# Second layer's transposes, derivative, keys, queries and values as one block with split products, and one preparation of expert weights less

## The reference, cut to what matters

```
exp_out = einsum('blef,edf->bled', gelu(einsum('bld,efd->blef', x, w1) + b1), w2) + b2   # first layer
...
lap_x = yp_x[:, :, :-2] - 2.0 * y + yp_x[:, :, 2:]      # second difference along the features
lap_y = yp_y[:, :-2, :] - 2.0 * y + yp_y[:, 2:, :]      # second difference along the tokens
du_dt = zX * lap_x + zY * lap_y + zR * y * (1.0 - y)
q, k, v = du_dt @ Wq.T, du_dt @ Wk.T, du_dt @ Wv.T      # then 4 heads, each with two softmaxes
...
```

## Time and profile before

| what | us |
|---|---|
| three runs | 1522.03, 1523.15, 1525.40 (median 1523.15) |
| the profiled execution, its own time | 1524.83 |
| its span (first to last instruction) | 1523.0 |
| busy: PE, DVE, ACT, POOL | 1372.9, 943.2, 722.7, 497.7 |
| last job's last VectorE instruction ends | 978.9 |
| last preparation on GpSimd ends | 983.6 |
| transposes of the second layer begin | 985.4 |
| `laplace_phase` begins | 991.8 |
| attention begins | 1053.8 |

### The profile page before, as it was taken

How to read it: one execution, slowest core, us unless ns; L and a number is a source line. 1 busy time by engine, 2 the same in 40 slices (tenths; PEclk the granted TensorE clock), 3 DMA queues, 4 the chain that set the end, 5 groups by cost and what they waited for, 6 DMA issues and landing times. The chain is left out here.

```text
span 1523.0 us, 24894 instructions
## 1 busy us (share of the span) xinstructions
PE 1372.9 (90%) x8678; PEld 1139.8 (75%) x8679; DVE 943.2 (62%) x1708; ACT 722.7 (47%) x1473; POOL 497.7 (33%) x478
## 2 busy tenths in 40 slices
PE   8866799978998789999999999888899899867998
PEld 3345356667895479999999999736688688647997
DVE  4955879965566854454343343395777777464776
ACT  3423877635122246555445556312555456333543
POOL 0331089830000234274062040442211210043885
PEclk9976989989998969999999999999999999988999
DMA  6000000010000014021011000050000000533550
GB/s 235 1 1 0 14 1 1 1 56 1 1 1 0 1 60 162 0 99 67 0 50 60 0 0 0 0 166 1 1 1 1 1 1 1 194 120 115 193 198 20
DMA packets 23244, 69.50 MB, mean 46 GB/s; under 512 B 4419, under 2 KB 8915, under 8 KB 18242
## 3 DMA queue, kind: packets, MB, share of 16 engines
q1 hardware_dynamic: 20866, 62.51, 11.8%
q0 software_dynamic: 2304, 6.03, 1.1%
HBM read 54.62 MB, written 14.19 MB: 45 GB/s over the span
## 5 line engine op out<-in xcount | busy, mean ns | idle before, releaser
L1702 DVE TENSOR_TENSOR ehidl<-hT,ehidh 128x512 fp32r<-128x512 f32 x148 | 140.4, 960 | 136.5 <-ACT ehidh L1685 135.9
L1679 ACT ACTIVATE hT<-ps,eb 128x256 f32<-128x256 f32 x296 | 124.4, 472 | 165.8 <-PE ps L1521 165.8
L2010 ACT ACTIVATE pr<-ps,nmax 128x256 f32<-128x256 f32 (+7 forms) x128 | 94.1, 739 | 103.4 <-DVE nmax L2040 103.3
L1521 PE MATMUL ps<-kh,qz 128*128 128x512 f32 (+3 forms) x384 | 125.3, 380 | 3.3 <-ACT pr L2010 1.9
L1709 DVE SCALAR_TENSOR_TENSOR X<-ps,wE,X 128x256 f32 x74 | 35.8, 484 | 108.3 <-PE ps L1521 98.7
L1685 ACT CAST ehidh<-hT 128x512 fp32r<-128x512 f32 x148 | 91.9, 621 | 4.7
L2040 DVE TENSOR_REDUCE nmax<-ps 128x1 f32<-128x256 f32 (+7 forms) x128 | 91.0, 748 | 1.2 <-PE ps L1950 0.6
L1603 POOL TENSOR_TENSOR eb<-eb1s,consts 128x8 f32<-128x8 f32 x8 | 2.1, 260 | 273.6 <-PE ps L1521 267.3
L1521 PEld LDWEIGHTS ps<-kh,qz 128*128 128x128 f32 x384 | 76.2, 199 | 13.3 <-ACT pr L2010 4.7
L1521 PE MATMUL ps<-ew_1h,ehidh 128*128 128x256 f32 x304 | 85.5, 281 | 0.5 <-POOL ew_1l L1623 0.5
L1521 PE MATMUL ps<-hTh,ew_1h 128*128 x304 | 85.4, 281 | 0.1
(11 more groups left out here) (524 smaller groups left out, 4303.1 us busy)
## 6 DMA issues: line engine op xcount, KB each, us to landing
ew1s<-in_ew_dram SPq DMA_DIRECT2D x9, 1024.0 KB, 4.7
ew2s<-in_ew_dram SPq DMA_DIRECT2D x9, 1024.0 KB, 6.8
fw1s<-in_fw_dram SPq DMA_DIRECT2D x8, 1024.0 KB, 7.6
fw2s<-in_fw_dram SPq DMA_DIRECT2D x8, 1024.0 KB, 9.4
slot_rows<-fill SPq DMA_DIRECT2D x1, 5140.0 KB, 20.1
xr<-slot_rows SPq DMA_DIRECT2D x8, 514.0 KB, 4.1
xT<-in_xT_dram SPq DMA_DIRECT2D x4, 512.0 KB, 7.6
X<-in_x_dram SPq DMA_DIRECT2D x1, 2048.0 KB, 18.2
```

The lines of the kernel that those rows point to most:

```text
L1521: last = nc.tensor.matmul(out, lhs[a], rhs[b], start=(start and n == 0), stop=(stop and n == 2), **kw)
L1679: nc.scalar.activation(hid[:, f, :], ps[:, f // 2, (f % 2) * JOB:(f % 2 + 1) * JOB], ACT.Gelu, bias=b1[q][:, f:f + 1]).then_inc(k.e_act, 1)
L1702: nc.vector.tensor_tensor(lo[:, f, :], hid[:, f, :], hi[:, f, :], ALU.subtract).then_inc(k.e_lo, 1)
L2010: nc.scalar.activation(pr[:, n % 3, u, 0:wide], half(n, u, wide), ACT.Exp, bias=nmax[:, n % 2, u:u + 1], accum_out=sums[:, u, n:n + 1]).th ...
```

## The change: what it does, and the diff

1. **Mixture.** GpSimd and SP handle expert 1 ahead of the loop, and the loop runs over max(pairs − 1, 1) further pairs, 2p+2 and 2p+3. With four pairs, GpSimd makes 7 preparations in place of 8 and SP one load less of each weight.
2. **One block.** The call of `transpose_phase` goes; `laplace_phase` does the transposes itself, window by window, and ScalarE alone copies them out (`stream`).
3. **Split products.** The stream, du, wk, wq and wv are each cut into high and low parts, and TensorE works with fp32r passes: four per second difference (2 halves × high and low; the constant matrix has one part), six per group of keys or queries (2 × `product3`) and twelve half-wide ones per group of values. The parts of the stream and of du share the buffers qh and ql, which the queries' parts later take.
4. **Who does what.** ScalarE makes all high parts and the growth factor (`growth`, z0·y + z1), and copies out the values, two tiles at once. VectorE makes low parts, the product with y, the neighbour sums (now straight from hT, `neighbours`) and the rest of du. GpSimd makes the weights' low parts first, clears a third of `qz` and the filler, waits for the last low part of du, clears the rest and places the queries.
5. **Order.** On PE, ACT and DVE the order is written out call by call; windows overlap.

```
-            return (p * 2 + 1, 1, p + 1) if q == 0 else (p * 2 + 2, 0, p + 2)
+            return p * 2 + (q + 2), q, p + 2
+        def later_pairs(eng, name):
+            rest = eng.alloc_register(f"{name}_later_pairs")
+            eng.reg_alu(rest, entry(eng, "pairs", 0, E0 // 2), -1, ALU.add)
+            eng.reg_alu(rest, rest, 1, ALU.max)
+            return eng.snap(rest, min_val=1, max_val=E0 // 2 - 1)
...
-            with pool.Fori(0, pairs) as p:
+            split(1, 1, 1)
+            with pool.Fori(0, rest) as p:
                 for q in range(2):
                     split(*following(p, q))
...
+            def second_difference(w, f):
+                pe.wait_ge(k.l_lap, 1)
+                pe.wait_ge(k.l_yl, EB * (w + 1))
+                for j in range(EB):
+                    for n in range(2):
+                        last = nc.tensor.matmul(ps[:, bank(w, f), :], lap[:, j * E + f * P:j * E + (f + 1) * P],
+                                                parts[n][:, j, window(w)], start=(j == 0 and n == 0),
+                                                stop=(j == EB - 1 and n == 1))
+            def keys(w, f):
+                pe.wait_ge(k.l_wl, SPLIT.index(KEY) + 1)
+                pe.wait_ge(k.l_dl, EB * (w + 1))
+                weighted(w, f, wk, k.l_km)
...
+            def high_weight(n):
+                act.wait_ge(k.s_wC, 16 * 4)
+                nc.scalar.copy(PARTS[n][0][:, :, :], WHOLE[n][:, :, :]).then_inc(k.l_wh, 1)
+            high_weight(0)
+            stream(0, 0)
+            high(0, 0)
+            stream(0, 1)
+            growth(0)
...
+            low_weight(0)
+            low_weight(2)
+            low_weight(1)
+            clear(0)
             nc.gpsimd.memset(k.fill[:, 0:ROWF - 1], 0.0).then_inc(k.z_fill, 1)
             nc.gpsimd.memset(k.fill[:, ID].bitcast(I32), OUTSIDE).then_inc(k.z_fill, 1)
+            pool.wait_ge(k.l_dl, EB * NW)
+            for q in range(1, QZ):
+                clear(q)
             pool.wait_ge(k.z_fill, 2)
-            pool.wait_ge(k.l_zero, 1)
+            pool.wait_ge(k.l_zero, 2 * QZ)
             pool.wait_ge(k.l_ql, EB)
             for i in range(QZ):
                 place_queries(nc, k, i)
...
+            def neighbours(w):
+                def add(at, of, n):
+                    o = du[:, :, first + at:first + at + n]
+                    then(nc.vector.scalar_tensor_tensor(o, k.hT[:, :, first + of:first + of + n], k.row("zy", b), o,
+                                                        ALU.mult, ALU.add))
...
-                transpose_phase(nc, k, k.X, k.hT, None, None, {"mm": k.t_5})
                 laplace_phase(nc, k)
```

More of the change, by code:

```diff
@@ L1762, in _ @@
[L1762 to L1782, removed]
-                last.then_inc(k.l_vm, 1)
+            def turn(w, f):
+                for j in range(4):
+                    last = nc.tensor.transpose(ps[:, bank(w, f), j * P:(j + 1) * P],
+                                               k.X[:, 4 * w + j, f * P:(f + 1) * P], k.const("ident"))
+                last.then_inc(k.t_5, 1)
@@ new lines, in weighted @@
+            def weighted(w, f, weight, done):
+                for j in range(EB):
+                    last = product3(nc, ps[:, bank(w, f), :], [x[:, j, f * P:(f + 1) * P] for x in weight],
+                                    [x[:, j, window(w)] for x in parts], j == 0, j == EB - 1)
+                last.then_inc(done, 1)
+            def keys(w, f):
+                pe.wait_ge(k.l_wl, SPLIT.index(KEY) + 1)
+                pe.wait_ge(k.l_dl, EB * (w + 1))
+                weighted(w, f, wk, k.l_km)
@@ new lines, in _ @@
+            second_difference(2, 1)
+            keys(1, 0)
+            keys(1, 1)
+            queries(0, 1)
+            second_difference(3, 0)
+            second_difference(3, 1)
+            values(1, 0)
+            keys(2, 0)
+            keys(2, 1)
+            queries(1, 0)
+            values(1, 1)
+            values(2, 0)
+            queries(1, 1)
+            keys(3, 0)
+            keys(3, 1)
+            queries(2, 0)
+            values(2, 1)
+            values(3, 0)
+            queries(2, 1)
@@ L1785, in _ @@
+            values(3, 1)
+            queries(3, 0)
+            queries(3, 1)
         @block.scalar
         def _(act):
[L1787 to L1802, removed]
+            def stream(w, f):
+                act.wait_ge(k.t_5, EB * w + f + 1)
+                nc.scalar.copy(k.hT[:, f, window(w)], ps[:, bank(w, f), :]).then_inc(k.l_ya, 1)
+            def high(w, f):
+                act.wait_ge(k.l_ya, EB * w + f + 1)
+                nc.scalar.copy(k.qh[:, f, window(w)], k.hT[:, f, window(w)]).then_inc(k.l_yh, 1)
@@ new lines, in _ @@
+            coefficients()
+            low(0, 0)
+            growth(0)
+            low(0, 1)
+            neighbours(0)
+            differences(0, 0)
+            differences(0, 1)
+            low(1, 0)
+            growth(1)
+            low(1, 1)
+            low_derivative(0, 0)
+            low_derivative(0, 1)
+            neighbours(1)
+            low_keys(0, 0)
+            differences(1, 0)
+            low(2, 0)
+            low_keys(0, 1)
+            low(2, 1)
+            growth(2)
```

272 lines of the change are left out of this document (203 added, 69 removed).

## The result

The changed kernel takes **1515.56 us** (median of five runs, 1513.12 to 1517.56) against 1523.15 (median of five as well): a ratio of 0.9951, with a 95% interval of 0.9939 to 0.9963, so 7.6 us less (5.6 to 9.3). Forecast were 1513.6 and a range of 1508.0 to 1519.5.

The account below looks back on a forecast made before the run. TensorE's list was taken to bound most of the program, with POOL alone holding the seam. 4.7 us at the seam plus 4.8 in the stretch (68.1 to 63.3) gave 9.5 off 1523.15: 1513.6 us, range 1508.0 to 1519.5.

Parts of the forecast that it names:

- Part 1: Seam behind the mixture: without POOL's unused last preparation, VectorE is last out, 4.7 us earlier; the following 1.8 us stay.
- Leg A: Block's start: ScalarE's first cast waits for four weight loads, so VectorE's first low part starts at 7.6 us.
- R3: Rival, walk too careful: loads land 1 us sooner, VectorE's waits vanish, block ends at 58.6, time 1508.9 us; chance 0.11.
- Leg B: VectorE's list up to window 2's derivative low parts: 27.8 us of work plus 3.7 of waits, ending at 39.1.
- The 1.1 for growth: VectorE's wait of 1.1 us behind ScalarE's growth step, which stands ahead of the next high part.
- the 1.6 at window 1's low part: VectorE's wait of 1.6 us for a high part made after growth and a weight cast, and against POOL's weight parts.
- a full lock: POOL's three weight low parts hold VectorE for their whole length, 3.7 us in place of 1.6; end at 65.4.
- Leg C: TensorE's last 15 groups, from keys(2, 0) on: 20.7 us plus 0.7 of waits, 21.4, ending at 60.7.
- R4: Rival, slower: TensorE stays at 1.2 GHz through its last 15 groups, 41.4 us for 20.7, result 1534; chance 0.04.
- Leg D: Block's end: POOL's placing of queries, 10.5 us from 52.7, ends last at 63.3, 0.5 us behind the rest.
- R2: Rival: the new lists mesh worse than the walk; the stretch takes 67.9 us, time 1518.2; chance 0.14.

Follow-up runs that it names:

- the block alone: The changed kernel with the mixture's old loops, so the preparation that no job reads is back: 1520.71 us, ratio 0.9971 to the kernel before.
- the second execution: The changed kernel unaltered, timed and profiled once more: 1516.99 us, ratio 0.9948 to the kernel before.
- the later cast: The changed kernel with ScalarE's cast of wk moved behind the copies of windows 0 and 1: 1513.34 us, ratio 0.9927 to the kernel before.
- The earlier placing: The changed kernel with ScalarE's high part of window 0's second half of queries moved ahead of the last two keys: 1515.01 us in one run.
- the last kernel: The changed kernel with wk's cast later, the queries step earlier, and 18 and 50 unused transposes in TensorE's pauses: 1510.17 us, ratio 0.9902 to the kernel before.

## Why the prediction held, step by step

**Part 1, the seam: 4.7 us.** Right to a tenth, and by its reason: the 1.8 us behind the last engine stayed, behind VectorE in each of the eleven profiled executions without the last preparation (1.76 to 1.77) and behind POOL in the block alone (1.79).

**Leg A: VectorE's first low part at 7.6.** It came at 6.5. The 4.4 us for the last load were carried over from the earlier trace rows; measured were 3.4 and, in the second execution, 4.2. This term was mis-sized by 1.0 us in one execution and 0.2 in the other. With 3.4 one half of R3 came true: ScalarE began 4.7 us behind the first transpose, before the 5 us that stood as R3's sign. The other half, that the waits vanish, did not. That the loads stand on the path is shown by the later cast (A from 6.5 to 1.9). Window 0's second difference began 10.4 and 11.2 us behind the first transpose, for 11 to 12.

**Leg B: 27.8 of work and 3.7 of waits.** VectorE's window has 28.3 of work in 31.1 us; 31.5 were forecast. The 1.1 for growth came out at 1.10. Of the 1.6 at window 1's low part only contention came true, 0.41 of lengthening: its high part was ready, and VectorE didn't wait for it. The 0.38 of idle time just ahead belong to the step on PSUM at 992.83, which waited for TensorE's second difference, whose passes stood 0.43 apart:

```profile
992.16 0.63 PE L1775 MATMUL ps<-ql,lapr 128*128 128x512 f32 x1
```
```profile
992.83 0.75 DVE L2015 SCALAR_TENSOR_TENSOR att<-ps,rows,att 128x512 f32<-128x512 f32 x1 [0.38 <-PE ps L1775]
```

**Contention.** VectorE's steps with two SBUF inputs were held (1.10 for 0.69; 4.75 for 2.86 with the cast later), its step on PSUM was not (0.75 at 991.70, under POOL's weight part), and the placing took 10.5 us, six sets of 1.70 or 1.71. That is the pattern of the Trainium skill (SBUF — State Buffer, "Who interferes with whom"), and this case's traces agree with it. The page excepts steps with one SBUF input in a 2-port mode, which the prediction left out when it told the rule, and the kernel before has steps with one SBUF input that were held:

```profile
991.83 3.59 DVE L1853 TENSOR_SCALAR zc<-rows 128x2 f32<-128x2 f32 x1 [0.31 <-PEq L434]
...
995.65 3.88 DVE L1831 TENSOR_SCALAR att<-hT,zc 128x512 f32<-128x512 f32 x1
...
1001.75 3.90 DVE L1831 TENSOR_SCALAR att<-hT,zc 128x512 f32<-128x512 f32 x1
...
1007.88 0.54 DVE L1831 TENSOR_SCALAR att<-hT,zc 128x512 f32<-128x512 f32 x1
```
```profile
995.65 3.59 POOL L1809 TENSOR_TENSOR nb<-hT 128x2044 f32<-128x2044 f32 x1
```

The 512-wide step takes 0.54 alone, and the one of two columns 0.17 in the changed kernel. The third was held by the clearing of `qz`, which only writes (999.66 to 1004.87). So some 10 of the 16.0 us in which the earlier trace rows show VectorE busy were holding, and "nearly full" was a misreading. The change takes this away: `growth` moves that step to ScalarE, and the neighbour sums and most of the clearing leave that stretch. A smaller edit, the kernel before with this step on ScalarE alone, was not run. An estimate from rows: at most the 2.3 us of TensorE's pause at 1005.8 (it waits there for du of window 0) and half of the 3.7 us at half clock, so some 4 us, near to the 4.4 that the new block gains in its second profile. Whether the new block was needed for its gain is therefore open.

The 3.7 us that the prediction allowed for by a full lock fell to 0.4. Of the three weight parts one met hardly any such step, one was held itself (2.18), and only the last held a low part; with GpSimd given the neighbour sums, the steps held, the waits for it and half clock made the block 4 to 6 us longer.

**Leg C: 21.4 us without half clock.** It took 21.5 (1016.59 to 1038.05), and 21.4 in the second execution. The granted clock was 1.00 in the last 20 us, TensorE busy 19.4 of 19.9; R4 is out for leg C. What the prediction had not priced is half clock ahead of it, in window 0's keys: 1.00 to 1.50 us of waiting on VectorE in most executions, and none in the first.

**Leg D: POOL's placing last, at 63.3, 0.5 behind VectorE.** It ended 61.9 us behind the first transpose in one execution and 63.6 in the other, and 0.5 behind VectorE in both. The earlier placing gives this 0.5 back. The margin is partly luck: the prediction lets placing start at 52.7 where its own terms give 50.5 + 2 × 0.62 + 0.68 = 52.4, and ends it at 63.2 or 63.3. Without these 0.4 the two ends fall together within 0.1.

**Sum.** Forecast 9.5. The profiles give 4.7 + 6.2 = 10.9 and 4.7 + 4.4 = 9.1, the medians 7.6 (5.6 to 9.3) and 7.9 (5.3 to 10.5). So the time lay inside the range, but 9.5 is just outside the first interval. R2's block (67.9) and R3's (58.6) were both missed by more than 3 us: 61.9 and 63.6. That the block came out within 1.4 us is in part errors of opposite sign: shorter loads (0.2 to 1.0) and a missing wait of 1.2 against half clock in window 0's keys (0 to 1.00 in these two). The first profile shows the block without that loss and is the fastest of its five runs. In the eight other kernels that have a ratio, the sum of seam and block lies between 1.9 above and 1.5 below the gain by it, so a loss elsewhere isn't shown. One source of scatter is attention itself. From its first VectorE step to the first one behind it, it took 248.3 us in the profiles of both kernels and 251.1 in the second execution of the changed one, but also 251.4 with the block alone, so it doesn't follow an edit.

## What to carry to other kernels

Joining a block that only feeds the next one pays through its loads: they start earlier, and its engines work under them; joining was worth the whole gain of the block here, the split products and the division of work, in this order, nothing without it. When work is handed to GpSimd, look at which VectorE steps run beside it: those with two SBUF inputs were held here, and so, in the kernel before, was a TENSOR_SCALAR with one (3.90 us for 0.54); those on PSUM weren't. A busy engine in a window can be an engine that is held: compare its steps with the same ones elsewhere. A cast that waits for a load belongs out of the front of an engine's list, though of the 4.5 to 5.4 us that this freed, 1.5 to 2.5 were given back to contention and to TensorE's clock. And one profile can be the favourable case: size a gain from two.

## What was not expected of the hardware

- TensorE's granted clock fell behind short pauses, and not always. In the changed kernel the same list had a pause of 2.10 us in one execution and of 2.18 in the other. In both the second differences ahead of it had run at 1.2 GHz (0.43 us apart) and the passes right behind it at 2.4; window 0's keys then ran at 2.4 GHz in the first, and at 1.2 in the second, where the clock fell at 1001.8. In the last kernel a pause of 0.28 us at the same place left it at 1.00, and so did one of 1.96 us ahead of window 0's second difference.
- The same four loads, issued one behind the other, landed 3.4 us or 4.2 us after the last issue in two executions of one kernel, and 3.4 to 4.8 us in all thirteen profiles. A stage that begins with a wait for them varies by that.
- Attention, untouched, takes 248.0 to 248.4 us in ten of the thirteen profiled executions and 251.1 to 251.4 in three (the second of the changed kernel, the block alone, the earlier placing). In exactly these three, TensorE's granted clock was 0.96 in place of 1.00 over the 40 us that begin 24 us into attention, and fewer matmuls fell into them. Here the first and then the second execution of the changed kernel:

```profile
1065.00:1105.00 40.00, 36.87 (x249) 30.43 (x248) 31.41 (x68) 21.90 (x60) 10.05 (x24) 1.00 0.01 1
```
```profile
1070.00:1110.00 40.00, 36.67 (x236) 30.15 (x235) 30.27 (x66) 20.94 (x57) 10.04 (x24) 0.96 0.01 1
```

Whether the clock is the cause or follows from something else was not tried.
